# A message-passing layer over sorted edges: the first 20 quads of edges by counts instead of gathers, and the spread matrices on ScalarE

## The chip, the cores and the metric

The kernel runs on one core of a Trainium2 chip. The metric is the device time of one execution in microseconds (us). The core has TensorE (PE, matmuls), VectorE (DVE), ScalarE (ACT), GpSimd (POOL) and SyncE (SP), which here only issues transfers, and 16 DMA engines that all queues share.

## The reference, cut to what matters

```python
h = jnp.maximum(_layernorm(x, axis=-1), 0.0)          # x: 12500 x 64
e = jnp.concatenate([h[src], h[dst]], axis=1)         # 200000 edges, dst sorted
m = jax.nn.relu(e @ W1 + b1) @ W2 + b2                # W1: 128 x 128, W2: 128 x 64
s = jax.ops.segment_sum(m, dst, num_segments=12500)
cnt = jax.ops.segment_sum(ones, dst, num_segments=12500)
out = x + s / jnp.maximum(cnt, 1.0)[:, None]
```

The edges are sorted by destination, and destinations are drawn as 12500·u², so the low nodes have very many edges each: the first 10,240 edges reach only some 33 nodes.

## The kernel before, in words

**Setup.** W1 is split in two halves, so that an edge's hidden row is relu(P[src] + q[dst]). The kernel first computes P and q for all 12,500 nodes (layer norm, a transposition, two products) and stores them as `p_table` and `q_table` in HBM, 128 float32 values to a row. It also turns `src` and `dst` so that 128 edges of a chunk lie on 128 partitions (`src_e`, `rel_e`), and writes `rel_table`, which holds each edge's destination relative to the first node of its window, as bfloat16 rows.

**Quads and couples.** 128 edges are a chunk, four chunks are a quad of 512 edges (391 quads), and two quads are a couple (196 couples). A couple is the step of the main loop. Neighbouring quads share a window of 128 nodes in groups of 4, 2 and 1 (199 groups).

**The gather.** For each chunk GpSimd issues one indirect DMA that fetches the 128 rows P[src] into the ring `g` of `RING = 36` quads (L485). Before it refills a slot, it waits at every fourth quad until TensorE has summed an earlier quad (`u_psum`, L483); how far it may run ahead falls from 36 to 8 quads. The first 10 quads (`RAW`) are not gathered from `p_table` but from x itself, early in the setup. The gathers of quads 10 to 35 begin as soon as `p_table` is stored, long before the main loop starts.

**One couple in the main loop** (`fast`, taken when every group's destinations fit into one window):
- SP loads two couples' relative destinations, repeated on all 128 partitions (512 KB, L414), and the q rows of each new window (64 KB, L409).
- VectorE compares them with the partition's number (`spread_of`, L802): a matrix of nodes times edges, and with it the edge counts of each node (`accum_out`).
- TensorE multiplies it with the window's q rows (`spread_q`, L1037): q[dst] for each edge, in PSUM (`z_all`, two buffers).
- VectorE makes the opposite matrix, edges times nodes (`members_of`, L809), waits for the gathered rows and adds them to q[dst] (`add_rows`, L820).
- ScalarE takes the relu (`relu`, L597), TensorE sums the rows to their nodes (`sum_edges`, L1050), and at a window's end ScalarE copies the sums (L603), TensorE multiplies them by W2 (L1057, L1068) and VectorE adds them to `sums` (`add_sums`, L830).
- Once the sums of 500 nodes are final, TensorE turns them (`turn_sums`, L1078), VectorE divides by the counts and adds x (`means`, L843), and SP stores the rows.

Each engine's instructions stand in the order in which Python writes them out; the engines meet only at semaphores.

Of the kernel before, what the change touches and what calls it, by code (L numbers as in the profile page):

```python
# [8 lines left out]
ALU = mybir.AluOpType  # L9
ACT = mybir.ActivationFunctionType  # L10
# [6 lines left out]
NP = 125  # L17
# [12 lines left out]
QE = 512  # L30
# [6 lines left out]
RING = 36  # L37
# [7 lines left out]
COUPLES = -(-QUADS // 2)  # L45
# [3 lines left out]
def groups():  # L49
    first, sizes = 0, []  # L50
# [8 lines left out]
GROUP = [i for i, quads in enumerate(GROUPS) for _ in quads]  # L59


def couple(m):
    return range(2 * m, min(2 * m + 2, QUADS))
# [9 lines left out]
BLOCK = [k for m in range(COUPLES) for k, groups_k in enumerate(BLOCKS) if GROUP[2 * m] in groups_k]  # L73
BLOCK_END = [GROUPS[groups_k[-1]][-1] // 2 for groups_k in BLOCKS]
# [37 lines left out]
MEAN_BLOCK = [min(BLOCK[last_quad(b) // 2] + 1, len(BLOCKS) - 1) for b in range(BATCHES)]  # L112
MEAN_AT = [BLOCK_END[k] + 2 for k in MEAN_BLOCK]
assert len(set(MEAN_AT)) == BATCHES
STORES = (0, 4, 8, 12, 16, 20, 23, 24, BATCHES)


def gnn_kernel(nc, x, src, dst, W1, b1, W2, b2, out):
    p_table = nc.dram_tensor("p_table", [NODES, HID], F32).ap()
    q_table = nc.dram_tensor("q_table", [NODES + WIN, HID], F32).ap()  # L120
    rel_table = nc.dram_tensor("rel_table", [QT * 128, QE], BF16).ap()

    ctx = ExitStack()
    with ctx:
# [6 lines left out]
        def sems(names):  # L131
# [5 lines left out]
        rows_f = sb("rows_f", [128, 1])  # L137
        eps = sb("eps", [128, 1])
# [9 lines left out]
        stats = sb("stats", [NP, NT, 6])  # L148
        two, diff, var, rstd, shift_n = (sb(n, [NP, NT]) for n in ("two", "diff", "var", "rstd", "shift_n"))
# [43 lines left out]
        g = sb("g", [128, RING, 4 * HID])  # L193
        slots = g[:, :, :].rearrange("p k c -> p (k c)")
        P_AT, UNIT_COLS = RAW * 512, 2 * UNIT * HID
        HT_AT = RING * 512 - PAIRS * NP
# [6 lines left out]


# [18 lines left out]
        columns_p = bank[7][:, 0:WIN]  # L223
        h_bank, rows_bank = bank[0:2], (bank[2:4], bank[4:6])
# [21 lines left out]
        v_zero, columns_done = sems("v_zero columns_done")  # L246
# [7 lines left out]
            "spread_done zq_done z_done r_done u_psum u_copied v_psum v_done")  # L254
        o_psum, most_done, inverse_done, mean_done, out_done = sems("o_psum most_done inverse_done mean_done out_done")


        windows_shifted, windows_counted, rows_in, rows_used, w_loaded, m_made, m_turned, m_spread, q_spread, z_made, \
            r_made, counted, u_made, u_moved, v_made, item_done, all_added = sems(
                "windows_shifted windows_counted rows_in rows_used w_loaded m_made m_turned m_spread q_spread z_made "  # L260
                "r_made counted u_made u_moved v_made item_done all_added")
# [38 lines left out]
        def slot(n):  # L300
            return n % RING
# [4 lines left out]
        def rows_of_p(m):  # L306

            k = slot(2 * m)
            return g[:, k:k + 2, :].rearrange("p k c -> p (k c)")[:, 0:HID * chunks_in(m)]
# [46 lines left out]
        def _(sp):  # L356
            def load_edges(what, to, loaded):
# [10 lines left out]
                         src[0:RAW * QE].rearrange("(n p c) -> p n c", p=128, c=4)).then_inc(idx_in, 16)  # L368
# [29 lines left out]
            def store_means(k):  # L398
                b, to = STORES[k], STORES[k + 1]
                tiles, s = pairs(xs[:, BT * b:BT * to, :]), slice(BT * b // 2, BT * to // 2)  # L400
                sp.wait_ge(mean_done, to)
# [3 lines left out]
            def load_window(i, first):  # L405
                k = i % WINDOWS
                if i >= WINDOWS:
                    sp.wait_ge(zq_done, GROUPS[i - WINDOWS][-1] // 2 + 1)
                sp.dma_start(qw[k], q_table[bass.ds(first, WIN), :]).then_inc(window_in[k], 16)  # L409

            def load_rows(j):
                if j >= 2:
                    sp.wait_ge(spread_done, parts_to(2 * (j - 1)))
                sp.dma_start(rows_of[j % 2], rel_table[4 * j:4 * j + 4, :].rearrange("(o q) e -> o (q e)", o=1)  # L414
                             .to_broadcast([128, 4 * QE])).then_inc(rows_there[j % 2], 16)

            def fast():
                stores = 0
                sp.wait_ge(rel_out, 16)
                for m in range(COUPLES):  # L420
                    if m % 2 == 0:
                        load_rows(m // 2)
                    for n in couple(m):
                        if n % 8 == 0:
                            firsts = first_nodes(sp, n)
                        if n == GROUPS[GROUP[n]][0]:
                            load_window(GROUP[n], firsts[n % 8])
                    if m == MEAN_AT[STORES[stores + 1] - 1] + 7:
                        store_means(stores)
                        stores += 1  # L430
                while stores < len(STORES) - 1:
# [3 lines left out]
            def general():  # L435
# [7 lines left out]
                for k in range(len(STORES) - 1):  # L443
# [3 lines left out]
            sp.wait_ge(out_done, 32 * (len(STORES) - 1))  # L447

        @block.gpsimd
        def _(pool):  # L450
# [22 lines left out]
            def gather(n):  # L473
                if n == RAW or n % 128 == 0:
                    pool.wait_ge(src_table, n // 128 + 1)
                if n == RAW_SLOT:
                    pool.wait_ge(raw_psum, RAW // 2)
                if n == HT_SLOT:
# [11 lines left out]
            def fast():  # L490
                for n in range(RING, QUADS):
# [14 lines left out]
            for n in range(RAW, RING):  # L506
# [4 lines left out]
        def _(act):  # L511
# [82 lines left out]

            def relu(m):
# [8 lines left out]

            def fast():
                for m in range(COUPLES + 1):
                    if m < COUPLES:
# [20 lines left out]
        def _(dve):  # L628
# [113 lines left out]
            for t in range(QT):  # L742
                nc.vector.tensor_scalar(limit[:, t:t + 1], rows_f[:, :], float(128 * t - LATE), 0.0,
                                        ALU.add, ALU.max).then_inc(limit_done, 1)
            dve.wait_ge(limit_done, QT)
# [8 lines left out]
            first = 0  # L754
# [8 lines left out]
            dve.wait_ge(base_done, len(GROUP_SIZES))  # L763
            for t in range(QT):
# [6 lines left out]
            nc.vector.scalar_tensor_tensor(worst[:, :], early[:, :], float(WIN), span[:, :],  # L771
                                           ALU.mult, ALU.add).then_inc(worst_done, 1)
# [21 lines left out]
            def spread_of(m):  # L794

# [353 lines left out]
```

## Time and profile before

| | |
|---|---|
| median of 3 runs | 1983.04 us (1981.84 to 1984.36) |
| span of the profiled execution, first to last instruction | 1978.7 us |
| TensorE, matmuls | 1262.6 us busy, 64% |
| VectorE | 866.2 us, 44% |
| ScalarE | 279.9 us, 14% |
| GpSimd | 1479.1 us, 75% |
| moved by DMA | 188.67 MB, mean 95 GB/s |

The page gives no time of the profiled execution beyond its span; the median of the timed runs is 4.3 us above the span. GpSimd's busy time is that of the instructions that issue the gathers; between two of them the engine's own overhead shows as idle time put down to "issue".

### The profile page before, as it was taken

The numbers are of one execution on the slowest core, as the hardware profiler recorded it, in microseconds if no ns is written. First come the engines' busy times: TensorE is split into PE (matmuls) and PEld (weight loads), VectorE is DVE, ScalarE is ACT, GpSimd is POOL, SyncE is SP. The second block draws the span as 40 slices with busy tenths as digits, with TensorE's granted clock in tenths as the row PEclk, the third lists the DMA queues.
The fourth block names the chain that finished last, engine by engine and source line by source line (L and its number), as shares of the span: only waits on it lengthen the run. The fifth ranks groups of instructions, "written<-read, shape, count | busy, mean of one in ns | idle before, by whom it ended". The sixth has DMA issues, their size and how long they took to land.

```text
span 1978.7 us, 20481 instructions
## 1 busy us (share of the span) xinstructions
PE 1262.6 (64%) x7608; PEld 1074.9 (54%) x7609; DVE 866.2 (44%) x1571; ACT 279.9 (14%) x429; POOL 1479.1 (75%) x1572
## 2 busy tenths in 40 slices
PE   5879555656566566565556665666666666766666
PEld 4768555555455555555545555555555555555554
DVE  9688433333333334343443433433343344444444
ACT  4232111111111111111111111111111111111111
POOL 7677777777777777777777777777777777777775
PEclk9889888887887888888888888888888788888888
DMA  8744223232323232333223233323232323233332
GB/s 193 227 131 126 89 76 89 77 88 77 89 77 92 79 93 80 92 91 92 80 84 88 82 92 90 93 80 93 80 102 80 96 84 112 85 101 86 105 89 53
DMA packets 122380, 188.67 MB, mean 95 GB/s; under 512 B 32448, under 2 KB 83943, under 8 KB 122275
## 3 DMA queue, kind: packets, MB, share of 16 engines
q0 software_dynamic: 50016, 101.22, 19.3%
q1 hardware_dynamic: 71695, 85.86, 14.3%
q8 instruction: 62, 1.02, 0.2%
q10 hardware_dynamic: 564, 0.23, 0.1%
q14 instruction: 43, 0.35, 0.1%
HBM read 170.59 MB, written 16.59 MB: 95 GB/s over the span
## 4 chain that ended last, share of the span: by engine, by line
POOL 70%; issue 23%; PE 2%; DVE 2%; DMA 1%; ACT 0%; SPq 0%; POOLq 0%; DVEq 0%; ACTq 0%
POOL g L485 70%; DMA g<-p_table,src_e 1%; DVE rows_b L680 1%; PE bank L1050 1%; PE z L1037 1%; DVE stats L664 0%; PE bank L933 0%; DVE work L802 0%; PE z L933 0%; PE bank L1068 0%; PE bank L1057 0%; PE z L926 0%; DVE acc L830 0%; DVE acc L636 0%; PE bank L1078 0%
## 5 line engine op out<-in xcount | busy, mean ns | idle before, releaser
L485 POOL DMA_INDIRECT g<-p_table,src_e x1523 | 1439.9, 945 | 470.5 <-issue 462.0
L820 DVE TENSOR_TENSOR g<-z,g 128x1024 f32<-128x1024 f32 x196 | 239.2, 1220 | 1059.1 <-DMA g<-p_table,src_e 1058.1
L1037 PE MATMUL z<-w,work 128*128 128x128 f32 x1558 | 300.3, 371 | 308.2 <-DVE work L802 307.5
L1037 PE MATMUL z<-work 128*128 128x128 f32 x1568 | 286.9, 358 | 306.6 <-DVE work L802 306.1
L1037 PEld LDWEIGHTS z<-w,work 128*128 128x128 f32 x1558 | 276.9, 276 | 325.1 <-DVE work L802 325.1
L1037 PEld LDWEIGHTS z<-work 128*128 128x128 f32 x1568 | 264.1, 263 | 323.7 <-DVE work L802 323.6
L597 ACT ACTIVATE g<-g 128x1024 f32<-128x1024 f32 x196 | 206.6, 1054 | 1609.2 <-DVE g L820 1609.2
L1050 PE MATMUL bank<-work,g 128*128 128x128 f32 x3126 | 415.5, 288 | 0.0
L1050 PEld LDWEIGHTS bank<-work,g 128*128 128x128 f32 x3126 | 382.5, 200 | 45.2 <-issue 45.2
L809 DVE TENSOR_TENSOR work<-bank,rel_e 128x1024 f32<-128x1024 f32 x196 | 238.7, 1218 | 6.6 <-PE bank L1050 3.7
L802 DVE TENSOR_SCALAR_CACHE_REDUCE work<-rel_q,rows_f 128x1024 f32<-128x1024 bf16 (+1 forms) x116 | 126.8, 1104 | 1.3 <-DMA rel_q<-rel_table 0.8
L802 DVE TENSOR_SCALAR_CACHE_REDUCE work<-rows_b,rows_f 128x1024 f32<-128x1024 bf16 (+2 forms) x115 | 126.0, 1106 | 0.0
L1057 PE MATMUL bank<-ident,count 128*1 128x128 f32 x462 | 97.8, 329 | 2.9 <-DVE acc L830 2.7
L1068 PE MATMUL bank<-sums_u,w 128*64 128x128 f32 (+1 forms) x328 | 93.9, 375 | 0.0
L1078 PE MATMUL bank<-fold,acc 65*125 65x65 f32 x200 | 31.6, 307 | 55.8 <-DVE acc L830 54.0
L1068 PEld LDWEIGHTS bank<-sums_u,w 128*64 128x64 f32 x328 | 37.0, 160 | 51.3 <-issue 50.7
L830 DVE TENSOR_TENSOR acc<-acc,bank 65x128 f32 x199 | 54.9, 276 | 14.0 <-PE bank L1068 9.4
L1078 PEld LDWEIGHTS bank<-fold,acc 65*125 65x125 f32 x200 | 27.9, 213 | 60.6 <-DVE acc L830 58.6
L1057 PEld LDWEIGHTS bank<-ident,count 128*1 128x1 f32 x462 | 27.9, 87 | 39.3 <-issue 20.3
L466 POOL DMA_INDIRECT g<-in_x_dram,idx_raw x40 | 38.0, 951 | 13.6 <-issue 11.9
L603 ACT COPY sums_u<-bank 128x128 f32<-128x128 f32 (+1 forms) x164 | 44.4, 271 | 2.8 <-PE bank L1050 1.8
L933 PE MATMUL bank<-w,g 128*125 128x256 f32 x100 | 28.1, 430 | 3.4 <-DVE work L717 3.4
(97 smaller groups left out, 315.1 us busy)
## 6 DMA issues: line engine op xcount, KB each, us to landing
rel_q<-rel_table SPq DMA_DIRECT2D x49, 512.0 KB
rows_b<-rel_table SPq DMA_DIRECT2D x49, 512.0 KB
g<-p_table,src_e POOLq DMA_INDIRECT x1523, 2.5
work<-q_table SPq DMA_DIRECT2D x100, 64.0 KB
w<-q_table SPq DMA_DIRECT2D x99, 64.0 KB
p_table<-g SPq DMA_DIRECT2D x12, 448.0 KB
q_table<-work SPq DMA_DIRECT2D x12, 448.0 KB
out_dram<-xs SPq DMA_DIRECT2D x5, 448.0 KB
```

What stands on the lines that cost most here:

```text
L485: nc.gpsimd.indirect_dma_start(out=g[:, slot(n), j * HID:(j + 1) * HID], out_offset=None, in_=p_table, in_offset=bass.IndirectOffsetOnAxis ...
L597: nc.scalar.activation(rows_of_p(m), rows_of_p(m), ACT.Relu).then_inc(r_done, 1)
L603: nc.scalar.copy(sums_u[:, k % 2, 0:w], u_bank[k % 2][:, 0:w]).then_inc(u_copied, 1)
L802: nc.vector.tensor_scalar(spreads[m % 2][:, at:at + w], rows_of[m // 2 % 2][:, row:row + w], rows_f[:, :], 0.0, ALU.is_equal, ALU.add, acc ...
L809: nc.vector.tensor_tensor(member[:, m % 2, :, :], columns_p.unsqueeze(1).to_broadcast([128, 8, WIN]), rel_e[:, 8 * m:8 * m + 8].unsqueeze( ...
L820: nc.vector.tensor_tensor(rows_of_p(m), z_all[m % 2][:, 0:HID * chunks_in(m)], rows_of_p(m), ALU.add)\
L830: nc.vector.tensor_tensor(v, v, v_bank[:, WIN * j:WIN * (j + 1)], ALU.add).then_inc(v_done, 1)
L1037: last = nc.tensor.matmul(z_all[m % 2][:, at:at + HID], spreads[m % 2][:, at:at + 128], qw[i % WINDOWS], start=True, stop=True)
L1050: last = nc.tensor.matmul(u_bank[k % 2][:, at:at + WIN], g[:, slot(n), HID * c:HID * (c + 1)], member[:, m % 2, 4 * (n % 2) + c, :], start ...
L1057: nc.tensor.matmul(v_bank[FEAT:FEAT + 1, at:at + WIN], count[:, j % COUNTS:j % COUNTS + 1], ident[:, :], start=j == parts[0], stop=j == pa ...
L1068: nc.tensor.matmul(v_bank[0:FEAT, 0:w], w2[:, :], sums_u[:, k % 2, 0:w], start=True, stop=True).then_inc(v_psum, 1)
L1078: last = nc.tensor.matmul(o[:, i, :], sums[:, first:first + 2 * NP - 1:2], fold[:, :], start=True, stop=True)
```

## The change

**The first 20 quads (`Q0 = 20`) are no longer gathered.** A node d has q[d] fixed, so the sum over its edges of relu(P[src] + q[d]) can be taken over sources instead: sum over all nodes s of count(s, d) · max(P[s], -q[d]), plus q[d] times the number of edges. For the `DENSE = 36` nodes that these quads can reach, the kernel now
- counts: each of 144 tallies (`TALLIES`; 4 per couple, couples 12 to 47) is a product on TensorE of two one-hot matrices, `high_hot` (128 x 125, made by VectorE) and `low_hot` (128 x 512, made by ScalarE in two passes, |x| and relu(1-|x|)). Five groups of seven or eight nodes are staged by ScalarE as 16-bit counts and stored in `tally_table`;
- turns P: for each of 13 spans of 1,024 nodes SP loads the rows of `p_table`, and TensorE turns them into PSUM (`turned`), hidden features on partitions;
- multiplies: for each span and each of the 36 nodes SP loads that node's 1,024 counts repeated on 128 partitions (256 KB), and VectorE does one `scalar_tensor_tensor` max(P, -q) · count with `accum_out` (`product_of`): 468 instructions, 432 of them 1,024 wide and 36 of them 212 wide, 4 per couple (8 for the narrow ones) in couples 54 to 166 of the new numbering;
- adds the result to `sums` before batch 0, whose means move to couple 170.

**The main loop** starts at quad 20: 186 couples, 194 groups. The ring has 28 slots in place of 36 (the memory above it holds the one-hots, counts and P rows). `z_all`'s second buffer becomes `turned`, so `spread_q` of a couple waits until `add_rows` of the couple before is done, and TensorE does it after `sum_edges` and not ahead of it.

**`spread_of` moves from VectorE to ScalarE** and becomes two passes over the couple: |row - partition|, then relu(1 - that) with the counts in `accum_out`.

**Setup** gets a check that the first 20 quads' destinations lie where the tallies expect them (otherwise the general branch is taken), some ten small instructions on VectorE.

```diff
-RING = 36
+SLOTS, RING = 36, 28
+Q0 = 20
-COUPLES = -(-QUADS // 2)
+COUPLES = -(-(QUADS - Q0) // 2)
...
 gather(n), GpSimd:
-                if n >= RING and n % 4 == 0:
-
-                    ahead = max(AHEAD_LEAST, RING - 4 * ((n - RING) // AHEAD_STEP))
-                    pool.wait_ge(u_psum, (n - ahead) // 2 + 2)
+                if r >= RING and r % 4 == 0:
+
+                    ahead = max(AHEAD_LEAST, RING - 4 * ((r - RING) // AHEAD_STEP))
+                    pool.wait_ge(u_psum, (r - ahead) // 2 + 2)
...
 SP:
+            def load_tallies(i, k, d):
+                if i >= BUFFERS:
+                    sp.wait_ge(product_done, i - BUFFERS + 1)
+                row = HIGH_DIGITS * d + SPAN // 512 * k
+                digits = -(-span_of(k) // 512)
+                sp.dma_start(tally_row[i % BUFFERS][:, 0:512 * digits],
+                             tally_table[row:row + digits, :].rearrange("(o a) b -> o (a b)", o=1)
+                             .to_broadcast([128, 512 * digits])).then_inc(tally_in[i % BUFFERS], 16)
...
+                for k, d in products_in(m - 2):
+                    load_tallies(DENSE * k + d, k, d)
...
 ScalarE:
+            def spread_of(m):
+
+                act.wait_ge(rows_there[m // 2 % 2], 16 * (m // 4 + 1))
+                at, w = 2 * QE * (m % 2), 128 * chunks_in(m)
+                nc.scalar.activation(spreads[m % 2][:, 0:w], rows_of[m // 2 % 2][:, at:at + w], ACT.Abs,
+                                     bias=minus_rows[:, :], scale=1.0).then_inc(far_done, 1)
+                act.wait_ge(far_done, m + 1)
+                at = 0
+                for k, i in enumerate(PARTS[m]):
+                    w = 128 * sum(chunks_of(n) for n in couple(m) if GROUP[n] == i)
+                    j = (parts_to(m) + k) % COUNTS
+                    to = spreads[m % 2][:, at:at + w]
+                    nc.scalar.activation(to, to, ACT.Relu, bias=1.0, scale=-1.0, accum_out=count[:, j:j + 1])\
+                        .then_inc(spread_done, 1)
+                    at += w
...
+            def far_low_of(p):
+
+                if p >= 2:
+                    act.wait_ge(low_hot_done, p - 1)
+                j = TALLIES[p][1]
+                nc.scalar.activation(far_low[p % 2], low_digits, ACT.Abs, bias=low_key[:, j:j + 1], scale=1.0)\
+                    .then_inc(far_low_done, 1)
+
+            def low_hot_of(p):
+                act.wait_ge(far_low_done, p + 1)
+                if p >= 8:
+                    act.wait_ge(tallied, p - 7)
+                nc.scalar.activation(low_hot[p % 8], far_low[p % 2], ACT.Relu, bias=1.0, scale=-1.0)\
+                    .then_inc(low_hot_done, 1)
...
 VectorE:
+            def high_hot_of(p):
+
+                if p == 0:
+                    dve.wait_ge(edge_keys, 5)
+                if p >= 8:
+                    dve.wait_ge(tallied, p - 7)
+                i, j = TALLIES[p]
+                nc.vector.tensor_scalar(high_hot[p % 8], columns_p[:, 0:125], high_key[:, j:j + 1],
+                                        float(-PER_GROUP * HIGH_DIGITS * i), ALU.subtract, ALU.is_equal).then_inc(high_hot_done, 1)
+
+            def product_of(i, k, d):
+
+                dve.wait_ge(tally_in[i % BUFFERS], 16 * (i // BUFFERS + 1))
+                dve.wait_ge(turned_done, k + 1)
+                w = span_of(k)
+                nc.vector.scalar_tensor_tensor(product[i % BUFFERS][:, 0:w], turned[:, 0:w], minus_q[:, d:d + 1],
+                                               tally_row[i % BUFFERS][:, 0:w], ALU.max, ALU.mult,
+                                               accum_out=parts_d[:, d, k:k + 1]).then_inc(product_done, 1)
...
             def fast():
-                spread_of(0)
...
                 for m in range(COUPLES + 4):
-                    if m + 1 < COUPLES:
-                        spread_of(m + 1)
                     if m < COUPLES:
...
                         members_of(m)
+                        for p in tallies(m):
+                            high_hot_of(p)
                         add_rows(m)
+                        dense(m)
...
 TensorE:
             def spread_q(m):
 
                 pe.wait_ge(spread_done, parts_to(m + 1))
+                if m:
+                    pe.wait_ge(z_done, m)
...
             def fast():
                 spread_q(0)
                 for m in range(COUPLES + 3):
-                    if m + 1 < COUPLES:
-                        spread_q(m + 1)
                     if 2 <= m < COUPLES + 2 and m - 2 == BLOCK_END[BLOCK[m - 2]]:
                         times_w2(BLOCK[m - 2])
                     if 1 <= m <= COUPLES:
                         sum_edges(m - 1)
+                    if m + 1 < COUPLES:
+                        spread_q(m + 1)
+                    dense(m)
```

TensorE's `dense(m)` is the four tallies of couple m - 1 (one bfloat16 matmul of 512 columns each), and in the couple before a span the eight transpositions of P, which wait for the last product of the span before.

## Rows read from the trace of the kernel before

**Rows 1.** The page's parts 1 and 4: busy time, and the chain of waits.
```profile
span 1978.7 us, 20481 instructions
...
POOL 70%; issue 23%; PE 2%; DVE 2%; DMA 1%; ACT 0%; SPq 0%; POOLq 0%; DVEq 0%; ACTq 0%
```
**Rows 2.** The groups by line: busy us, mean ns of one, idle before it and releaser.
```profile
L485 POOL DMA_INDIRECT g<-p_table,src_e x1523 | 1439.9, 945 | 470.5 <-issue 462.0
...
L820 DVE TENSOR_TENSOR g<-z,g 128x1024 f32<-128x1024 f32 x196 | 239.2, 1220 | 1059.1 <-DMA g<-p_table,src_e 1058.1
...
L597 ACT ACTIVATE g<-g 128x1024 f32<-128x1024 f32 x196 | 206.6, 1054 | 1609.2 <-DVE g L820 1609.2
...
L809 DVE TENSOR_TENSOR work<-bank,rel_e 128x1024 f32<-128x1024 f32 x196 | 238.7, 1218 | 6.6 <-PE bank L1050 3.7
L802 DVE TENSOR_SCALAR_CACHE_REDUCE work<-rel_q,rows_f 128x1024 f32<-128x1024 bf16 (+1 forms) x116 | 126.8, 1104 | 1.3 <-DMA rel_q<-rel_table 0.8
```
**Rows 3.** The same view, smaller groups: forms like those that the change adds.
```profile
L843 DVE SCALAR_TENSOR_TENSOR xs<-bank,inverse,xs 125x64 f32<-125x64 f32 x100 | 21.5, 277 | 0.9
...
L737 DVE SCALAR_TENSOR_TENSOR real<-acc 128x512 f32<-128x512 f32 x1 | 0.7, 680 | 0.0
...
L785 DVE TENSOR_TENSOR rel_e<-z,base 128x512 f32<-128x512 f32 x4 | 4.0, 1068 | 0.2 <-PE z L918 0.2
...
L549 ACT COPY g<-bank 125x512 f32<-125x512 f32 x13 | 7.0, 590 | 6.9 <-PE bank L933 6.3 <-issue 0.6
```
**Rows 4.** The waits: who waited for whom, us in total, times, longest.
```profile
DVE g L820 <- DMA g<-p_table,src_e: 1058.1, 178, 7.0
...
POOL g L485 <- PE bank L1050: 1.8, 6, 0.3
```
**Rows 5.** Stretches: length; PE, PEld, DVE, ACT, POOL busy (count); clock; DMA share; GB/s.
```profile
60.00:70.00 10.00, 7.78 (x25) 6.36 (x26) 5.70 (x10) 0.60 (x1) 7.61 (x8) 0.66 0.85 256
...
500.00:510.00 10.00, 4.16 (x21) 3.78 (x19) 3.56 (x4) 1.21 (x2) 7.55 (x8) 0.75 0.22 57
510.00:520.00 10.00, 7.23 (x54) 6.07 (x54) 3.75 (x5) 1.06 (x1) 7.55 (x8) 0.91 0.38 109
...
600.00:800.00 200.00, 121.54 (x728) 104.92 (x727) 76.59 (x108) 23.74 (x37) 151.24 (x161) 0.82 0.30 86
```
**Rows 6.** The timeline of the setup: start, us, instruction; gathers and VectorE beside them.
```profile
60.26 1.44 POOL L485 DMA_INDIRECT g<-p_table,src_e  x1 [6.66 <-DMA p_table<-g]
...
81.78 1.22 DVE L705 TENSOR_TENSOR g<-g,r_rstd 128x1024 f32<-128x1024 f32 x1
81.98 1.84 POOL L485 DMA_INDIRECT g<-p_table,src_e  x1 [0.30 <-issue]
```
**Rows 7.** The timeline where the main loop begins: the second couple's sum of edges.
```profile
132.74 1.95 PE L1050 MATMUL bank<-work,g 128*128 128x128 f32 x16
```
**Rows 8.** The timeline of one couple, far into the loop.
```profile
503.85 1.23 DVE L820 TENSOR_TENSOR g<-z,g 128x1024 f32<-128x1024 f32 x1 [6.13 <-DMA g<-p_table,src_e]
504.99 1.27 DVE L802 TENSOR_SCALAR_CACHE_REDUCE work<-rows_b,rows_f 128x1024 f32<-128x1024 bf16 x1
506.19 1.22 DVE L809 TENSOR_TENSOR work<-bank,rel_e 128x1024 f32<-128x1024 f32 x1
...
506.32 3.78 PE L1037 MATMUL z<-work 128*128 128x128 f32 x16 [5.84 <-DVE work L802]
...
510.98 0.69 PE L1068 MATMUL bank<-sums_u,w 128*64 128x128 f32 x2
...
511.60 2.16 PE L1050 MATMUL bank<-work,g 128*128 128x128 f32 x16
...
513.86 1.23 DVE L820 TENSOR_TENSOR g<-z,g 128x1024 f32<-128x1024 f32 x1 [6.45 <-DMA g<-p_table,src_e]
```
**Rows 9.** The timeline of the end: the last gather and the last transfer.
```profile
1963.11 0.94 POOL L485 DMA_INDIRECT g<-p_table,src_e  x1 [0.30 <-issue]
...
1976.53 0.67 SPq L403 DMA_DIRECT2D out_dram<-xs  x1
```

More of the change, by code:

```diff
@@ L1 @@
+import math
 from contextlib import ExitStack
@@ L109, in last_quad, with near @@
     return n
-MEAN_BLOCK = [min(BLOCK[last_quad(b) // 2] + 1, len(BLOCKS) - 1) for b in range(BATCHES)]
-MEAN_AT = [BLOCK_END[k] + 2 for k in MEAN_BLOCK]
+MEAN_BLOCK = [min(BLOCK[couple_of(last_quad(b))] + 1, len(BLOCKS) - 1) for b in range(BATCHES)]
+BEFORE, AFTER = 0.75, 1.75
+def near(n):
+    first = math.ceil(RISE * max(n - BEFORE, 0) ** 2 - 1 - 0.01)
+    return range(max(first, 0), math.floor(RISE * (n + AFTER) ** 2 + 0.01) + 1)
+DENSE = max(near(n)[-1] for n in range(Q0)) + 1
+NC = 4 * Q0
@@ new lines, with tallies @@
+HIGH_DIGITS = -(-NODES // 512)
+PER_GROUP = 125 // HIGH_DIGITS
+DGROUPS = -(-DENSE // PER_GROUP)
+TALLIES = [(i, 4 * n + c) for i in range(DGROUPS) for n in range(Q0) for c in range(4)
+           if near(n)[0] < PER_GROUP * (i + 1) and near(n)[-1] >= PER_GROUP * i]
+TALLY_FIRST = [min(p for p, (i, _) in enumerate(TALLIES) if i == k) for k in range(DGROUPS)]
+TALLY_LAST = [max(p for p, (i, _) in enumerate(TALLIES) if i == k) for k in range(DGROUPS)]
+ROUND_TALLIES, TALLY_ROUND = 4, 12
+def tallies(m):
+    first = ROUND_TALLIES * (m - TALLY_ROUND)
+    return range(max(first, 0), max(min(first + ROUND_TALLIES, len(TALLIES)), 0))
@@ L114, with span_of @@
+def span_of(k):
+    return SPAN if k < SPANS - 1 else TAIL
+MEAN_AT_OF = [BLOCK_END[k] + 2 for k in MEAN_BLOCK]
+MEAN_AT_OF[0] = PRODUCT_LAST + 4
+while MEAN_AT_OF[0] in MEAN_AT_OF[1:]:
+    MEAN_AT_OF[0] += 1
+assert DENSE <= BT * NP and MEAN_AT_OF[0] < COUPLES
+ORDER = sorted(range(BATCHES), key=lambda b: MEAN_AT_OF[b])
+MEAN_AT = [MEAN_AT_OF[b] for b in ORDER]
 assert len(set(MEAN_AT)) == BATCHES
-STORES = (0, 4, 8, 12, 16, 20, 23, 24, BATCHES)
+STORED = (0, 4, 8, 12, 16, 20, 23, 24, BATCHES)
@@ L118, in gnn_kernel @@
+STORES = sorted((1 + max(ORDER.index(b) for b in range(first, to)), first, to) for first, to in zip(STORED, STORED[1:]))
 def gnn_kernel(nc, x, src, dst, W1, b1, W2, b2, out):
@@ L907, in general @@
                 dve.sem_inc(all_added, 1)
-                for b in range(BATCHES):
-                    means(b)
+                for i in range(BATCHES):
+                    means(i)
             if_one_window(dve, fast, general)
@@ new lines, in turn_p @@
+            def turn_p(k):
+                pe.wait_ge(p_rows_in, 16 * (k + 1) if k < SPANS - 1 else 16 * (k + 2))
+                if k:
+                    pe.wait_ge(product_done, DENSE * k)
+                else:
+                    pe.wait_ge(tally_staged, DGROUPS)
+                for j in range(-(-span_of(k) // 128)):
+                    rows = min(128, span_of(k) - 128 * j)
+                    last = nc.tensor.transpose(turned[:, 128 * j:128 * j + rows], p_rows[0:rows, j, :], ident[0:rows, 0:rows])
+                last.then_inc(turned_done, 1)
```

353 lines of the change are left out of this document (276 added, 77 removed).

## The prediction

> **What bounds the kernel now.** I read the page's chain of waits first: 70% of it is GpSimd and 23% is "issue" [rows 1], and the groups by line say what both are: 1523 indirect gathers at L485, 945 ns each, with 462.0 us of "issue" between them [rows 2]. 0.945 + 462.0/1523 = 1.248 us per gather, 10.0 us per couple of eight. The waits confirm it from the other side: VectorE's `add_rows` stood 1058.1 us for gathered rows, while GpSimd waited for TensorE 1.8 us in all [rows 4]. The gathers run from 60.26 us to 1963.11 us without a break; before them lies the setup, behind them a tail of 1978.7 - 1963.1 = 15.6 us [rows 6, 9]. So a removed gather is worth 1.248 us, if everything else keeps within 10.0 us per couple. The question is whether it does: all other engines have spare time now (VectorE 3.6 us of ten, ScalarE 1.1 to 1.2) [rows 5], and the change spends it.
>
> **What it removes.** 20 quads of 4 gathers: 80 · 1.248 = 99.9 us off GpSimd's stream. The 10 quads that come from x stay 10, so the start at 60.3 us stays. The rest of those ten couples' work on the other engines goes too, off the path.
>
> **GpSimd's own waits.** The ring shrinks from 36 to 28 quads. The first refill now comes after 18 quads · 4 · 1.248 = 90 us, at about 151 us, and asks for two couples to be summed. Before, that had happened at 132.74 + 1.95 = 134.7 us [rows 7]; with the new order (two ScalarE passes of about 1.06 us, the width of L597 [rows 2], ahead of the first product, and ScalarE's zeroing before them) I expect about 140 us. Cover 11 us; if the first sums came later than 151 us, the difference would be lost one to one. Later the permitted lead in quads falls to 8, that is, a gather waits for the couple three before its own. Its rows have then been there for about 17 us; a couple's chain behind `add_rows` (1.2), relu (1.1), spread product on cold TensorE (3.8), times W2 (0.7 + 1.0) and sum (2.2) [rows 2, 8] is 10 us, so about 7 us stay.
>
> **VectorE per couple.** It loses L802 and gains products. The form (float32 from PSUM, a 16-bit tensor from SBUF, a scalar by pointer, an accumulator) is not in the trace. From below: nothing excludes half of L820's time, 0.6 us for 1,024. Nearest rows: L820 reads PSUM and SBUF over 1,024 columns in 1.22 us, and L737, the same operation from SBUF, 512 in 0.68, so 1,024 in about 1.21 [rows 2, 3]; L802 with its accumulator advances 1.20 us (504.99 to 506.19) [rows 8]. From above: L785, a form that takes 1068 ns for 512 [rows 3], 2.2 us for 1,024. I take 1.25, nearest to L820. A product couple is then 4 · 1.25 + 1.22 + 1.22 + 0.3 (`add_sums`) = 7.7 us, with means now and then 1.2 more: under 10.0. All in, VectorE does 432 · 1.25 + 36 · 0.45 + 144 high one-hots · 0.28 = 597 us more and, for L802 and ten couples, about 296 us less: about 1167 us busy. It stays hidden, since `add_rows` waits 6.1 to 6.5 us per couple today [rows 8]. Without that cover each us over 10.0 in the 113 product couples would cost 113 us.
>
> Behind a product burst wait `add_sums` and the next `members_of` (both ahead of the next `add_rows`), for which 2 us are left. TensorE's transpositions at a span's end wait for the burst's last product; `sum_edges` behind them comes some 7 us after `add_rows` in place of 4 or so, 12 times, still within the couple.
>
> **ScalarE per couple.** Two passes of 1.06 for the spread, 1.06 for relu, 0.25 for the copy: 3.5 us. In the 36 tally couples eight passes of 512 columns, 0.59 each from L549 [rows 3], 4.7 more: 8.2 us. From below 8 · 0.48 (half a pass of 1,024 with no start cost, and some) = 6.1 or so in sum, from above eight passes as long as a 1,024-wide one, 8 · 1.06 + 3.5 = 12.0. I take 8.2 to 9, under 10.0. ScalarE's spread for the couple after next is made well before `add_rows` releases TensorE, so nobody waits. Busy in all: 280 + 186 · 2.12 + 288 · 0.59 less ten couples = about 835 us.
>
> Today's ScalarE groups with no pointer operand take 1054 ns for 1,024 columns and 590 for 512 [rows 2, 3]. The Trainium skill (ScalarE: Activation LUTs, What ACT_TABLE_LOAD costs) says that a bias by pointer adds about 93 ns to an ACTIVATE; no run here shows it yet. By that rule a tally couple would come to an estimated 9.1 us, still under ten, so the sum would not change.
>
> **TensorE.** The spread product may not run ahead any more; it starts when `add_rows` ends. It takes 2.1 to 3.8 us and the next `add_rows` is 10.0 us away [rows 8], so it ends 6 us early. A couple needs 3.8 + 1.7 + 2.2 = 7.7 us there [rows 8]. The four tallies are 2,048 columns, as many as the 16 records of 128 in those 3.8 us, but bfloat16: no row has that type, so 3.8 us from above and a quarter of it, 0.9, from below. I take 1.9: 9.6 us, no wait. At the upper end 36 couples would fall 54 us behind, which the ring's lead of some five couples about hides.
>
> **Transfers.** 432 loads of 256 KB and 36 narrow ones come to about 115 MB, 1 MB more per product couple. Steady traffic has the DMA engines busy 30% at 86 GB/s; the ten us with a 512 KB load have 0.38 and 109 GB/s against 0.22 and 57 without [rows 5], so 0.16 per 52 GB/s, and 105 GB/s more give about 0.62. At 0.85 and 256 GB/s in the setup eight gathers still took 7.61 us of issue in ten us, against 7.55 later [rows 5]. From below zero cost. From above, if the packets cost twice that, 0.94: still not full. SP must issue four more transfers of 0.33 us, and each waits for the product six before, so window and row loads queue behind them about three couples ahead of their use: covered by some 20 us. I cost them at nothing.
>
> **Setup and tail.** A gather is stretched when VectorE works beside it with both operands in SBUF: 1.84 us in place of 0.94 beside L705 [rows 6]; beside L820 it is not (the mean of 1523 is 945 [rows 2]). The products have the form of L820 and L843 in this, one operand in PSUM. The check and the keys are some twenty small ones of 0.16 to 0.3 us: 0 to 5 us, I take 1. The Trainium skill (SBUF — State Buffer, Who interferes with whom) says that VectorE in a two-port mode holds the pair that it shares with GpSimd for the whole instruction; by its rule the four instructions that fill `low_digits` are of that kind, and would add an estimated 1 us, which the sum can do without. The tail is the same chain, with the last spread product a little later: -0.5 to +1.5, I take 0.
>
> **The sum.** Span: 1978.7 - 99.9 + 1 = 1879.8 us; the runs' median lies 4.3 us above the span of before, so 1884.1 us. Bounds of this case: 1879 to 1891.
>
> **The rivals.**
> A, a VectorE bound. Place: couples 54 to 166. If a product takes the 2.2 us of L785's rate, a couple is 8.8 + 2.7 = 11.5 us, 1.5 above; over 113 couples +170 us, less some 20 us of lead: 1884 + 150 = 2034 us, slower. It starts above (10.0 - 2.7)/4 = 1.8 us per product and is slower than before from 2.1 us. For it: nothing shows this operand mix. Against: L820, L737 and L843 all run a column a cycle. 6%.
> B, gathers stretched by the products. If each of 468 products held a gather as L705 did, 0.9 us, no gain would be left: +421 us, 2305; if one in four, +105, 1989, slower or level. Against: 196 L820 and 196 L809 stretched none. 3%.
> C, ScalarE in the tallies. At 12.0 us a couple, 36 couples lose 72 us; the ring lets the loop fall back some five couples, 50 us, before GpSimd stands: 1884 + 22 = 1906. 6%.
> D, small stalls. VectorE's burst, means, the transpositions at span ends and late transfers fall together in some couples, and where the lead is 8 quads (couples 134 on) GpSimd stands a few us: 33 product couples · 0.5 to 1 us, about 1910 with the rest. For it: 2 us are left in a product couple. 12%.
> E, the change doesn't do what it says: a window or the check fails, and the general branch runs, one quad at a time: 391 · (5.0 us of gathers + the 10 us chain), some 5900 us. 1%.
>
> **How the numbers follow.** The forecast holds 72%; C and D, 18% together, are faster too: 90%. Within 0.2% (4 us, about what a measurement of this kernel can tell from no change) 2%, out of the milder ends of A and B; slower the other 8% of A, B and E. The range is 1877 to 1922: the case's own 1879 to 1891, widened downwards by the tail and upwards over C and D.
>
> **What would show it.** Right: 1443 gathers at 945 ns, a chain with over 90% GpSimd and issue, L485's wait for TensorE under 10 us, product groups near 1.25 us, VectorE near 1170 us and ScalarE near 835 us busy, DMA share about 0.6 in the middle. Wrong: a wait of L485 for L1050 of tens of us (then the start says the ring, couples 12 to 47 say ScalarE, couples 54 to 166 VectorE), or a mean of L485 above 950.

## The result, and the profile after

The changed kernel takes 1883.36 us (1880.9 to 1886.26, 4 runs) against 1983.7 us of the kernel before in the same comparison: ratio 0.9497 (0.9483 to 0.951). Forecast was 1884.1 us.

The page of the changed kernel: lines of its parts 1, 4 and 5. The gather is now L644, `add_rows` L1047, the products L1107, the two passes of the spread L758 and L766, those of the tallies L785 and L792:

```profile
span 1881.3 us, 23045 instructions
...
PE 1266.5 (67%) x7535; PEld 1076.8 (57%) x7536; DVE 1182.1 (63%) x2189; ACT 858.0 (46%) x1346; POOL 1403.2 (75%) x1492
...
POOL 60%; issue 23%; PE 12%; DVE 3%; DMA 1%; ACT 0%; SPq 0%; DVEq 0%; POOLq 0%; ACTq 0%
...
L644 POOL DMA_INDIRECT g<-p_table,src_e x1443 | 1364.2, 945 | 447.8 <-issue 438.3
L1107 DVE SCALAR_TENSOR_TENSOR g<-z,norms,g 128x1024 bf16<-128x1024 f32 (+1 forms) x468 | 541.8, 1214 | 6.7 <-DMA g<-tally_table 6.7
L1047 DVE TENSOR_TENSOR g<-z,g 128x1024 f32<-128x1024 f32 x186 | 226.8, 1220 | 474.6 <-DMA g<-p_table,src_e 462.3
L1099 DVE TENSOR_SCALAR g<-bank,norms 128x125 bf16<-128x125 f32 x144 | 42.4, 345 | 104.2 <-PE z L1381 102.5
L758 ACT ACTIVATE work<-rel_q,minus_rows 128x1024 f32<-128x1024 bf16 x94 | 107.2, 1140 | 0.0
L785 ACT ACTIVATE g<-g,norms 128x512 bf16<-128x512 f32 x144 | 99.7, 716 | 2.4
L792 ACT ACTIVATE g<-g 128x512 bf16<-128x512 bf16 x144 | 85.0, 613 | 0.0
```

Read against [rows 2]: a gather costs what it did, 945 ns, and there are 80 fewer. VectorE's wait for gathered rows fell from 1058.1 to 462.3 us: that is where the 468 products went. The source line of the gathers and the end of the timeline give the account (start, duration, waits; last gather and last transfer):

```profile
L644 POOL DMA_INDIRECT g<-p_table,src_e x1443: 940/944/1865, 61.7 to 1864.4; - x181
...
  issue: 438.3, 1438
  DMA p_table<-g: 8.3, 1
  PE bank L1338: 1.2, 4
```
```profile
1864.41 0.94 POOL L644 DMA_INDIRECT g<-p_table,src_e  x1 [0.30 <-issue]
...
1879.28 0.45 SPq L515 DMA_DIRECT2D out_dram<-xs  x1
```

The stream of gathers is 1802.7 us long in place of 1902.8, 100.1 less; it starts 1.4 us later (61.7 for 60.3) and the tail behind the last gather is 16.9 in place of 15.6 us, 1.3 more. -100.1 + 1.4 + 1.3 = -97.4, which is the difference of the spans. GpSimd waited 1.2 us for TensorE.

Busy time by stretch, columns as in [rows 5]: the tally couples (200 to 400 us) and the product couples.

```profile
200.00:300.00 100.00, 72.03 (x474) 60.00 (x472) 44.95 (x79) 98.80 (x157) 75.61 (x81) 0.91 0.32 90
300.00:400.00 100.00, 68.75 (x409) 58.67 (x410) 36.61 (x67) 85.15 (x138) 75.47 (x81) 0.85 0.31 86
...
1000.00:1200.00 200.00, 132.47 (x766) 113.55 (x765) 149.22 (x238) 67.88 (x100) 151.23 (x161) 0.79 0.69 199
```

In each, GpSimd is busy 75.5 of 100 or 151.2 of 200 us, as before [rows 5], whatever the others do: ScalarE is 99% busy from 200 to 300 us, VectorE 75% and the DMA engines 0.69 later on. The 99% is the loop catching up with gathers that began long before it: from 200 to 300 us the rows lie ready, VectorE's `add_rows` waits 1.1 us for them (34.2 us in the next 100), and ScalarE sets the pace, at less than 10 us a couple.

### The profile page after: what moved, and what is told of

Read it like the earlier page. It is cut to its first block, busy times and chain, and to the rows that moved or that the text cites. A ratio compares the mean times of both kernels' runs of the same rounds, so it can differ in the third digit from the quotient of the medians.

```text
span 1881.3 us, 23045 instructions
## 1 busy us (share of the span) xinstructions
PE 1266.5 (67%) x7535; PEld 1076.8 (57%) x7536; DVE 1182.1 (63%) x2189; ACT 858.0 (46%) x1346; POOL 1403.2 (75%) x1492
## 4 chain that ended last, share of the span: by engine, by line
POOL 60%; issue 23%; PE 12%; DVE 3%; DMA 1%; ACT 0%; SPq 0%; DVEq 0%; POOLq 0%; ACTq 0%
POOL g L644 60%; PE z L1325 4%; PE bank L1338 3%; PE bank L1356 1%; PE z L1219 1%; PE bank L1345 1%; DVE rows_b L897 1%; DVE norms L881 1%; PE bank L1219 1%; PE bank L1367 1%; DMA g<-p_table,src_e 0%; PE bank L1263 0%; DMA rel_q<-rel_table 0%; DVE g L1047 0%; DMA g<-tally_table 0%
## 5 line engine op out<-in xcount | busy, mean ns | idle before, releaser
L644 POOL DMA_INDIRECT g<-p_table,src_e x1443 | 1364.2, 945 | 447.8 <-issue 438.3
L1107 DVE SCALAR_TENSOR_TENSOR g<-z,norms,g 128x1024 bf16<-128x1024 f32 (+1 forms) x468 | 541.8, 1214 | 6.7 <-DMA g<-tally_table 6.7
L1047 DVE TENSOR_TENSOR g<-z,g 128x1024 f32<-128x1024 f32 x186 | 226.8, 1220 | 474.6 <-DMA g<-p_table,src_e 462.3
L1338 PE MATMUL bank<-work,g 128*128 128x128 f32 x2966 | 466.7, 322 | 0.7
L1325 PE MATMUL z<-w,work 128*128 128x128 f32 x1440 | 240.1, 335 | 166.4 <-issue 128.2
L1325 PEld LDWEIGHTS z<-w,work 128*128 128x128 f32 x1440 | 224.3, 245 | 177.6 <-issue 155.6
L766 ACT ACTIVATE work<-work 128x1024 f32<-128x1024 f32 (+2 forms) x221 | 202.5, 916 | 5.9
L758 ACT ACTIVATE work<-rel_q,minus_rows 128x1024 f32<-128x1024 bf16 x94 | 107.2, 1140 | 0.0
L758 ACT ACTIVATE work<-rows_b,minus_rows 128x1024 f32<-128x1024 bf16 x92 | 105.4, 1145 | 0.0
L785 ACT ACTIVATE g<-g,norms 128x512 bf16<-128x512 f32 x144 | 99.7, 716 | 2.4
L792 ACT ACTIVATE g<-g 128x512 bf16<-128x512 bf16 x144 | 85.0, 613 | 0.0
```

The source lines that it names most:

```text
L644: nc.gpsimd.indirect_dma_start(out=g[:, slot(n), j * HID:(j + 1) * HID], out_offset=None, in_=p_table, in_offset=bass.IndirectOffsetOnAxis ...
L758: nc.scalar.activation(spreads[m % 2][:, 0:w], rows_of[m // 2 % 2][:, at:at + w], ACT.Abs, bias=minus_rows[:, :], scale=1.0).then_inc(far_ ...
L766: nc.scalar.activation(to, to, ACT.Relu, bias=1.0, scale=-1.0, accum_out=count[:, j:j + 1])\
L785: nc.scalar.activation(far_low[p % 2], low_digits, ACT.Abs, bias=low_key[:, j:j + 1], scale=1.0)\
L1047: nc.vector.tensor_tensor(rows_of_p(m), z[:, 0:HID * chunks_in(m)], rows_of_p(m), ALU.add)\
L1107: nc.vector.scalar_tensor_tensor(product[i % BUFFERS][:, 0:w], turned[:, 0:w], minus_q[:, d:d + 1], tally_row[i % BUFFERS][:, 0:w], ALU.ma ...
```

## The experiments

All ratios are to the kernel before, run beside each of these on the same chip, so they compare with 0.9497. Unless another time is named, the kernel before took 1987.76 us there.

**One part of the change alone: the spread on ScalarE, in the kernel before.** The definition of `spread_of` goes with the calls, in its ScalarE form of two passes.
```diff
 ScalarE, fast():
+                spread_of(0)
                 for m in range(COUPLES + 1):
+                    if m + 1 < COUPLES:
+                        spread_of(m + 1)
 VectorE, fast():
-                    if m + 1 < COUPLES:
-                        spread_of(m + 1)
```


> The kernel before with one part of the change alone: the spread matrices in two passes on ScalarE, all else as before (36 ring slots, two buffers of z, all 391 quads gathered). My theory is that the stream of 1523 gathers at 1.248 us sets the time and everything else lies beside it: 1983 us as before, within 3, VectorE about 250 us less busy, ScalarE about 450 more. Rival 1, a part of the 100 us came from the shorter VectorE couple: 1960 us or less. Rival 2, ScalarE's two passes lie on the path at the start or the end: 1987 to 1995.


Measured: 1986.16 us against 1987.76, ratio 0.9992 (0.9982 to 1.0001). VectorE is 634.7 us busy for 866.2, ScalarE 718.0 for 279.9. Taking 231.5 us of work off VectorE is worth nothing by itself, and the 438 us that it costs ScalarE cost no time: both engines had it.

**That part undone in the changed kernel: the spread back on VectorE.**
```diff
 ScalarE, fast():
-                spread_of(0)
...
-                    if m + 1 < COUPLES:
-                        spread_of(m + 1)
 VectorE, fast():
+                    if m + 1 < COUPLES:
+                        spread_of(m + 1)
```


> The changed kernel with the spread matrices back on VectorE, all else as changed. A product couple on VectorE is then 4 x 1.20 + 1.14 + 1.21 + 0.2 + 1.2 = 8.6 us, and 9.7 with means. My theory: under 10.0, so 1883 us within 4, VectorE about 1430 us busy. Rival (small stalls, that ScalarE's part was needed to make room): means, the transpositions and a burst fall together, some 25 couples lose 1 to 2 us that the lead of 8 quads can't give back: 1900 to 1930 us, with GpSimd waiting for TensorE tens of us.


Measured: 1886.02 us, ratio 0.9492 (0.9476 to 0.9508). Two of the waits of this kernel (who for whom, us, times, longest):
```profile
POOL g L644 <- issue: 438.9, 1440, 0.3
DVE g L1039 <- DMA g<-p_table,src_e: 363.5, 119, 8.7
```
VectorE is 1406.8 us busy and still waits 363.5 us for rows; GpSimd waited 0.6 us for TensorE. So the move to ScalarE was not needed at four products per couple, and the rival of small stalls falls even with 1.2 us less room per couple.

**The dense work left out.** Tallies, counts, transpositions and products go, and with them the first 20 quads' share of the result.
```diff
-                    dense(m)            # SP, ScalarE, VectorE and TensorE
-                        for p in tallies(m):
-                            high_hot_of(p)
```


> The changed kernel without tallies, stores and loads of counts, transpositions and products: the first 20 quads' share of the result is left out. My theory, all of that work is hidden: 1883 us within 3, landing of a gather back at 2.5 us. Rival (the dense work costs some us in small stalls or by its transfers, and the gathers removed are worth more): 1870 to 1878. Rival 3 (the first 20 quads' removal is worth less than 100 us by itself): 1890 or more.


Measured: 1888.53 us, ratio 0.9504 (0.9488 to 0.952): within the 0.2% that the intervals leave, the dense work costs nothing. The span, 1885.2 us, is even 3.9 us above the changed kernel's; 3.6 us of that are the gathers themselves, which took 947 ns in place of 944 in the median in this execution (1406.8 for 1403.2 us of GpSimd's busy time):
```profile
L643 POOL DMA_INDIRECT g<-p_table,src_e x1443: 943/947/1785, 60.5 to 1866.6; - x181
...
DMA to landing us min/median/max: 2.4/2.5/4.5
```
The landing is back at 2.5 us; with the dense work its median was 3.3, and that cost no time.

**A smaller ring.**
```diff
-SLOTS, RING = 36, 28
+SLOTS, RING, ABOVE = 36, 20, 28
```
(`ABOVE` keeps the one-hots and counts where they were.)


> The changed kernel with 20 ring slots in place of 28. GpSimd's first refill comes after 10 quads, at about 61.7 + 50 = 112 us, and asks for two couples summed, which the changed kernel has at 137.5 us. My theory (a wait of the gather stream counts one to one): 25 us of wait at the start, 1908 us, and nothing later, though the lead falls to 8 quads earlier. Rival 1, the ring's size doesn't bind, since the stream catches up: 1883. Rival 2, the shorter lead costs in the tally and product couples too: 1920 or more.


Measured: 1912.23 us, ratio 0.9622 (0.9606 to 0.9638), that is (0.9622 - 0.9497) · 1987.76 = 24.8 us over the changed kernel. GpSimd waited 24.9 us for TensorE, and its timeline shows 23.94 of them in one piece:
```profile
111.90 0.95 POOL L644 DMA_INDIRECT g<-p_table,src_e  x1 [0.30 <-issue]
136.79 0.95 POOL L644 DMA_INDIRECT g<-p_table,src_e  x1 [23.94 <-PE bank L1338]
```
A wait of the gather stream counts one to one, and only the start waits.

**Each product twice.** The ring has 24 slots here and in the two kernels with loads twice and products from SBUF, to make room; by the rule of the smaller ring that costs some 6 us.
```diff
+                if i >= 2:
+                    dve.wait_ge(spare_done, i - 1)
+                nc.vector.scalar_tensor_tensor(spare[:, i % 2, 0:w], turned[:, 0:w], minus_q[:, d:d + 1],
+                                               tally_row[i % BUFFERS][:, 0:w], ALU.max, ALU.mult,
+                                               accum_out=spare_sum[:, i % 2:i % 2 + 1]).then_inc(spare_done, 1)
```


> The changed kernel with a second product of the same form before each (its result thrown away into two spare ring slots, so the ring has 24 slots; by the wait at 20 slots I expect some 6 us for that alone). A product couple on VectorE is then 8 x 1.20 + 1.14 + 1.21 + 0.2 = 12.2 us, 2.2 over the gathers' 10.0, in 113 couples, and the means and TensorE's part of them (1.2 and some 3.5 us) are no longer hidden in about 14 of these. My theory: 1884 + 6 + 245 + 65 less 20 of lead, about 2180 us, slower than before: VectorE sets the time between couples 54 and 166, and GpSimd waits for TensorE. Rival (only the sum of VectorE's busy time counts, since it has time left elsewhere: 1182 + 560 = 1742 us of 1881): 1890 to 1930.

> The changed kernel with each product preceded by a second one of the same form, 24 ring slots, again on another chip. A product couple on VectorE is 12.2 us. My theory (VectorE sets the time in couples 54 to 166): 245 us more, plus 65 for means no longer hidden, plus 6 for the ring, less 20: about 2180 us, ratio 1.10, and a rate of 12.2 us or a little more per couple in that stretch. Rival (VectorE's busy total counts, 1742 us of 1881): ratio 0.95 to 0.97.


Measured the second time, against 1985.96 us of the kernel before: 2172.35 us, ratio 1.0942 (1.0924 to 1.096), 2180 expected. GpSimd's largest wait besides issue, two product stretches (columns as in [rows 5]), and `add_rows` from 800 to 1600 us:
```profile
POOL g L647 <- PE bank L1346: 301.8, 50, 31.0
```
```profile
1000.00:1200.00 200.00, 112.55 (x598) 97.18 (x599) 194.32 (x315) 54.95 (x80) 119.69 (x127) 0.74 0.56 157
1200.00:1400.00 200.00, 112.32 (x602) 96.25 (x601) 193.69 (x318) 54.72 (x78) 105.88 (x112) 0.74 0.53 155
```
```profile
L1050 DVE TENSOR_TENSOR g<-z,g x63: 1202/1212/1219, 806.5 to 1587.7; 128x1024 f32<-128x1024 f32 x63
```
VectorE is 97% busy and does 63 couples in these 800 us: (1587.7 - 806.5)/62 = 12.6 us per couple, where 12.2 or a little more were expected. GpSimd issues some 480 gathers in the same time, 13.3 us for each couple's eight. That is slower than VectorE's couples because its permitted lead, by the kernel's own rule, shrinks from 16 to 8 quads in this stretch. It waits 301.8 us in all. VectorE is only 1708 us busy of 2170: the share over the whole span did not decide, the stretch did. This is the mechanism of the prediction's rival A, brought about; the 2180 us worked out for this kernel were 8 us too many.

**One step further: 24 quads by counts.**
```diff
-Q0 = 20
+Q0 = 24
...
-ROUND_TALLIES, TALLY_ROUND = 4, 12
+ROUND_TALLIES, TALLY_ROUND = 4, 6
...
-ROUND_PRODUCTS = 4
...
-SPAN_ROUNDS = [-(-DENSE // ROUND_PRODUCTS)] * (SPANS - 1) + [-(-DENSE // (2 * ROUND_PRODUCTS))]
+SPAN_ROUNDS = [9] * 8 + [10] * 4 + [5]
```


> One step further: 24 quads by counts, 51 nodes, 663 products, six per couple, tallies from couple 6, product spans of 9 or 10 couples. 16 gathers less: -20.0 us. A product couple on VectorE is 6 x 1.20 + 1.14 + 1.21 + 0.2 = 9.75 us, with means and their wait 14: over 72 couples some 24 us behind, which the lead of 16 to 28 quads covers; in the later spans every tenth couple is free of products. My theory: 1864 us within 5. Rival (VectorE or the transfers, 0.86 busy, can't be hidden any more): 1885 or more.

> The kernel with 24 quads by counts (51 nodes, 663 products, six per couple) again, on another chip: on the first one TensorE's instructions came late in every kernel, 0.3 to 2.4 us apart inside one sum of edges, and the kernel before took 2441 us, so that the gathers did not set the time there. Expected as before: 20 us less than the changed kernel, ratio to the kernel before 0.940 (1864 of 1984) if all of the products stay hidden; 0.950 or more if VectorE's couple of 9.75 us or the transfers do not.


Measured the second time, against 1985.96 us: 1871.09 us, ratio 0.9424 (0.9408 to 0.944). It beats both kernels: 0.9424/0.9497 is 0.992, 14.5 us less than the changed one, where 20 were expected. Its gathers, and one stretch:
```profile
L643 POOL DMA_INDIRECT g<-p_table,src_e x1427: 940/944/1977, 62.1 to 1851.5; - x179
...
  PE bank L1337: 9.8, 10
```
```profile
1000.00:1200.00 200.00, 126.08 (x756) 110.77 (x755) 189.88 (x307) 69.60 (x100) 151.23 (x161) 0.80 0.85 247
```
With VectorE 95% busy and the DMA engines at 0.85 the gathers still keep their pace; 8.6 of the 9.8 us of waiting come after 1400 us, where the lead is shortest. 20.0 - (9.8 - 1.2) = 11.4 us is the span's gain by that, 1881.3 - 1868.5 = 12.8 the measured one. So at six products per couple GpSimd begins to wait.

**Loads twice, and products that read SBUF.** Both runs of each, and the first runs of the two kernels above, fell under a condition in which the kernel before takes 2441 or 2481 us.
```diff
+                sp.dma_start(spare[:, i % 4, 0:512 * digits],        # loads_twice: the same counts again
...
 VectorE, products_sbuf:
-                nc.vector.scalar_tensor_tensor(product[i % BUFFERS][:, 0:w], turned[:, 0:w], minus_q[:, d:d + 1],
+                nc.vector.scalar_tensor_tensor(product[i % BUFFERS][:, 0:w], spare[:, 0:w], minus_q[:, d:d + 1],
```


> The changed kernel with every load of counts issued a second time, into four spare ring slots (24 slots left, some 6 us). The DMA engines were busy 0.67 in the product couples against 0.31 without, so the share would be 1.03. My theory, that transfers were hidden with little to spare, makes them the bound now: at least 0.3 us more per couple, 1925 to 1970 us. Rival (the share counts overlapping packets and the engines have more to give): 1890, with a longer landing only.

> The changed kernel with each load of counts issued twice, 24 ring slots, again on another chip. My theory, transfers were hidden with little to spare: the DMA share of the product couples goes from 0.67 to 1.0, so a couple takes 10.4 us or more: 1925 to 1970 us, ratio 0.97 to 0.99. Rival (the engines have more to give than the share says, only the landing grows): 1890, ratio 0.953.

> The changed kernel with the products reading old data of two spare ring slots in place of the turned P in PSUM (so the first 20 quads' share of the result is wrong), 24 ring slots. Both tensors of a product now come from SBUF, as in the setup's instruction beside which a gather took 1.84 us in place of 0.94. Theory of the prediction's rival B: four such products hold two to four gathers of each couple by up to 0.9 us, 113 couples: +200 to +400 us, 2090 to 2290. Rival: that stretch needs something else than two operands in SBUF, and the time is 1890 as with 24 slots alone.

> The changed kernel with the products reading two spare ring slots in SBUF in place of the turned P in PSUM (the first 20 quads' share of the result is wrong), 24 ring slots, again on another chip. There GpSimd's issuing instructions were busy 1597 us in place of 1403, so a theory of the port says: the gathers of the product couples are stretched by some 195 us in all and, as they set the time on this chip, it comes to 1884 + 6 + 195 = 2085 us, ratio 1.05. Rival, the stretch falls in GpSimd's idle time between two gathers or is made up: 1890, ratio 0.953.


Measured there:

| kernel | us | kernel before | ratio |
|---|---|---|---|
| loads twice | 2477.32 | 2440.71 | 1.0132 (1.0108 to 1.0157) |
| loads twice, again | 2531.92 | 2480.73 | 1.0206 (1.0175 to 1.0238) |
| products from SBUF | 2528.42 | 2440.71 | 1.0374 (1.0329 to 1.0418) |
| products from SBUF, again | 2554.95 | 2480.73 | 1.0281 (1.0229 to 1.0334) |
| each product twice | 2590.14 | 2440.71 | 1.0609 (1.058 to 1.0639) |
| 24 quads | 2512.26 | 2440.71 | 1.029 (1.0268 to 1.0313) |

TensorE's own instructions came late there. One sum of edges of the 24-quad kernel begins like this in the timeline:
```profile
600.88 0.27 PE L1337 MATMUL bank<-work,g 128*128 128x128 f32 x1 [1.83 <-issue]
...
601.61 0.35 PE L1337 MATMUL bank<-work,g 128*128 128x128 f32 x1 [0.46 <-issue]
...
604.40 0.37 PE L1337 MATMUL bank<-work,g 128*128 128x128 f32 x1 [2.44 <-issue]
```
The gathers did not set the time (GpSimd waited 566.3 us for TensorE in this kernel), so neither question was settled. Whether doubled loads cost anything stays open: the share was 0.80, not 1.03, in product stretches that ran a third slower.

That the SBUF form can hold a gather is plain all the same. The kernel with loads twice is its control: measured beside it, same ring, same condition, products from PSUM. The gathers' source lines, loads twice first:
```profile
L651 POOL DMA_INDIRECT g<-p_table,src_e x1443: 938/944/1377, 98.4 to 2455.4; - x181
```
```profile
L645 POOL DMA_INDIRECT g<-p_table,src_e x1443: 942/947/5741, 98.9 to 2481.4; - x181
```
With products from PSUM no gather that ran beside a product took over 0.97 us, here or in the changed kernel. With products from SBUF 94 of the 1443 gathers took more than 1.05 us, 33 of them more than 4. The timeline of GpSimd and VectorE:
```profile
998.99 5.71 POOL L645 DMA_INDIRECT g<-p_table,src_e  x1 [0.30 <-issue]
...
999.00 1.27 DVE L1108 SCALAR_TENSOR_TENSOR g<-g,norms 128x1024 bf16<-128x1024 f32 x1
...
1000.20 1.27 DVE L1108 SCALAR_TENSOR_TENSOR g<-g,norms 128x1024 bf16<-128x1024 f32 x1
...
1001.40 1.27 DVE L1108 SCALAR_TENSOR_TENSOR g<-g,norms 128x1024 bf16<-128x1024 f32 x1
...
1002.61 1.27 DVE L1108 SCALAR_TENSOR_TENSOR g<-g,norms 128x1024 bf16<-128x1024 f32 x1
...
1013.54 2.18 POOL L645 DMA_INDIRECT g<-p_table,src_e  x1 [0.31 <-issue]
...
1015.98 1.31 DVE L1108 SCALAR_TENSOR_TENSOR g<-g,norms 128x1024 bf16<-128x1024 f32 x1
1016.03 0.95 POOL L645 DMA_INDIRECT g<-p_table,src_e  x1 [0.30 <-issue]
```
The first of these gathers begins 10 ns before a burst of four products and lasts over the whole burst, which ends at 1003.9, and 0.8 us beyond: 5.71 us in place of 0.94. But the hold is not a rule for every burst. Two bursts later a gather is through after 2.18 us, the next one runs its usual 0.95 beside the third product, and 270 of the 357 gathers that ran beside such a product took no more than 1.05 us. What decides it is not shown. Over the kernel GpSimd was 1596.6 us busy, 195 more than in the control (1401.7), and 1599.2 in the second run. If the gathers set the time and were held as often, an estimated 195 us would be about twice the change's gain; no run here shows that.

## Why the prediction was right

**The bound.** The cost and the path were right: 80 gathers at 1.248 us were to go, and 100.1 us of the stream went. The changed kernel, the one with the spread back on VectorE and the one without any dense work lie at 0.9497, 0.9492 and 0.9504: the removal is the whole gain. One of the signs that were named did not come: the chain was to be over 90% GpSimd and issue, and it is 83% with 12% TensorE, since from about 1670 us on the page follows it along TensorE. Why it leaves GpSimd there is not shown. That does not speak against the bound, since GpSimd waited 0.3 us for TensorE from 1600 us to the end.

**The ring.** The second couple was to be summed at about 140 us, against a refill at 151; it was at 135.54 + 1.95 = 137.5 us:
```profile
135.44 1.87 PEld L1338 LDWEIGHTS bank<-work,g 128*128 128x128 f32 x16
135.54 1.95 PE L1338 MATMUL bank<-work,g 128*128 128x128 f32 x16
```
With 20 slots the same rule gave 25 us and 24.9 were waited.

**VectorE.** A product was taken at 1.25 us; one starts 1.20 after the other, and each record is 1.27 long:
```profile
1007.40 1.27 DVE L1107 SCALAR_TENSOR_TENSOR g<-z,norms,g 128x1024 bf16<-128x1024 f32 x1
...
1008.60 1.28 DVE L1107 SCALAR_TENSOR_TENSOR g<-z,norms,g 128x1024 bf16<-128x1024 f32 x1
```
L820's rate held for the new operand mix, and rival A needed 1.8. The busy total came to 1182 us for 1167; its terms were further off than that. The forecast took 296 us off for L802 and ten couples; the kernel with only the spread moved shows 231.5 for the first, and ten times L820 and L809 are 25, so 256. The products were 542 us and not 556, and part of the new work overlaps in the records.

**ScalarE.** 858 us for 835. Most of the 23 us is the spread: it was put at 2.12 us a couple, and the kernel with only the spread moved paid 438/196 = 2.23. A tally couple was put at 8.2 us from rows. The first passes of the couples from 200 to 300 us, when ScalarE was 99% busy, give its true pace:
```profile
L758 ACT ACTIVATE work<-rel_q,minus_rows x7: 1131/1132/1133, 200.6 to 297.9; 128x1024 f32<-128x1024 bf16 x7
L758 ACT ACTIVATE work<-rows_b,minus_rows x6: 1131/1133/1134, 216.7 to 289.7; 128x1024 f32<-128x1024 bf16 x6
```
13 couples begin in 297.9 - 200.6 = 97.3 us, 8.1 us each. The records of one couple add up to 4 · (0.716 + 0.613) + 1.14 + 1.05 + 0.19 + 1.05 + 0.27 = 9.0 us, but neighbouring records overlap by some 0.1 us. So 8.2 came out right by two slips that offset each other: it left out what pointers and the accumulator's read add, and it counted the overlaps twice. The Trainium skill (ScalarE: Activation LUTs, What ACT_TABLE_LOAD costs) gave 93 ns per pointer operand, and the 103 and 86 ns here (716 and 1140 ns against 613 and about 1054 without) agree. The 9.1 us that the prediction estimated from it is the sum of the records; as the pace of a couple the 8.2 was nearer.

**TensorE.** Four tallies were taken at 1.9 us a couple; the 144 were 46.0 us in all, 1.3 for four.

**Transfers.** The share was 0.69 for a forecast of 0.62, and the landing 3.3 us for 2.5 before. That the gathers keep their pace at 0.85 was read from the setup and is shown by the 24-quad kernel in the loop.

**The port.** The prediction put rival B at 3% since L820 and L843 have one operand in PSUM. That was the right row to look at, since beside products that read PSUM no gather was stretched. The price was off in both ways. It took 0.9 us for each product from L705, 421 us in all; with products from SBUF a single hold was up to 4.8 us, but only some bursts held a gather, and the total was 195 us. The Trainium skill (SBUF — State Buffer, Who interferes with whom) says that a VectorE instruction with two inputs in SBUF contends with a GpSimd instruction that reads SBUF; the 5.71 us agree with that, and so do the 944 ns beside products that read PSUM. The gathers that were not held beside products from SBUF show that contention does not lengthen each of them. The estimated 1 us for the instructions that fill `low_digits` did not show: six gathers took over 1.05 us, 2.6 us more than usual together, against five and 2.7 before.

**What was luck.** The bound and the covers were right; that the forecast of 1884.1 us lies 0.7 us from the measured median was luck. The setup was put at +1 and the tail at 0 us, and they came at +1.4 and +1.3, so the span was 1881.3 for 1879.8. The 4.3 us between span and median offset that: the median is 2.1 us above the span of the changed kernel, and each of its four runs is 1.8 or 1.9 us longer than its own span, so most of the 4.3 us came of an execution of the kernel before that was faster than its timed runs. Nor does the +1.4 bear out the term for the check. The first gather of `p_table` starts at 60.3 to 62.1 us in the kernels measured under the usual condition, and at 62.1 in the one with only the spread moved, which has no check.

## What to carry to other kernels

Where one engine issues without a pause and nothing else ever makes it wait, its instruction count is the time: work may go to the other engines, as long as each stretch, not the average, stays under that engine's pace or is short enough for the lead to cover. Put a price per loop step on every engine and find the step at which the next one takes over (1.8 us per product by the prediction's sum; eight products of 1.2 us in place of four were over it). And ask of each new VectorE instruction beside a GpSimd stream where both of its inputs lie: the same operation stretched no gather from PSUM and held one for up to 5.7 us from SBUF.

## What the runs showed of the hardware

- A burst of four VectorE instructions with both inputs in SBUF, 1.20 us apart, could hold an indirect DMA's issue for 5.71 us in place of 0.94. It did so in some bursts: 33 of 1443 issues took over 4 us. With one input in PSUM none beside a product took over 0.97.
- The issue of a gather took 944 ns in the median in some executions and 947 in others, which alone is some 4 us of a span here, 0.2%.
- On two occasions, on chips with different numbers, the kernel before took 2441 and 2481 us instead of 1984. The number of the second had given 1987.76 us earlier the same day, so this is not shown to be a trait of a chip, and its cause stays open. Matmuls stood 0.46 to 2.44 us for "issue" inside a sum of edges, and GpSimd stood 45.1 us for the stored `p_table` (loads twice), against 8.3 in the changed kernel. The changed kernel itself was not run there; the 24-quad kernel was 2.9% slower than the kernel before, so the gain shown here holds where the gathers set the time.
